# Nine row copies with their own semaphores, and a one-tensor tie step, in stage 1 of an eight-stage transformer kernel

## The reference, cut to what matters

```
att = einsum(q, k) / sqrt(8), causal
S = relu(att[head 0]); S[..., 0] = 0; S = S * (1 - eye)
FF = cumsum(S shifted down one row, axis=rows)       # T x T
att = att - FF                                        # every head
keep = rank of FF in its row (ties by index) < eff_k, or the diagonal
att = where(keep, att, -inf); y = softmax(att) @ v; out = y @ w_proj.T + b
```

## Time and profile before

| | us |
|---|---|
| median of 3 runs | 2910.46 |
| lowest, highest run | 2904.49, 2914.45 |
| the profiled execution's own time | 2907.81 |
| its span in the profile | 2906.0 |

### The profile page before, as it was taken

How to read it: one execution, slowest core, us unless ns; L and a number is a source line. 1 busy time by engine, 2 the same in 40 slices (tenths; PEclk the granted TensorE clock), 3 DMA queues, 4 the chain that set the end, 5 groups by cost and what they waited for, 6 DMA issues and landing times. The chain is left out here.

```text
span 2906.0 us, 73996 instructions
## 1 busy us (share of the span) xinstructions
PE 2553.9 (88%) x30564; PEld 1586.3 (55%) x30564; DVE 1802.5 (62%) x5184; ACT 1796.3 (62%) x3222; POOL 347.1 (12%) x718
## 2 busy tenths in 40 slices
PE   7989788888888999999997999999999999886586
PEld 3668466665665532122113657667667676564355
DVE  6899788777875651000005577787787778653852
ACT  3799565555665269999993266666667667421331
POOL 3100332222220100000000100000000000034025
PEclk8989799999999999999998999999999999897698
DMA  3410001111002011100000000000000000312103
GB/s 118 71 26 2 7 12 17 17 17 17 17 10 55 1 59 54 56 1 1 1 1 17 28 14 8 8 2 7 7 2 8 8 2 2 98 23 40 29 19 55
DMA packets 85111, 68.12 MB, mean 23 GB/s; under 512 B 40776, under 2 KB 73688, under 8 KB 84392
## 3 DMA queue, kind: packets, MB, share of 16 engines
q1 hardware_dynamic: 76328, 57.09, 8.2%
q0 software_dynamic: 8448, 6.30, 1.7%
HBM read 47.21 MB, written 19.96 MB: 23 GB/s over the span
## 5 line engine op out<-in xcount | busy, mean ns | idle before, releaser
L1890 ACT ACTIVATE arena<-ps 128x1024 f32<-128x1024 f32 x512 | 474.1, 1281 | 25.9 <-PE ps L1840 24.0
L1341 DVE CUSTOM_DVE_ANT_0 arena<-ps,arena 128x1024 f32<-128x1024 f32 (+7 forms) x384 | 349.9, 931 | 107.0 <-PE ps L1217 91.1
L2268 DVE CUSTOM_DVE_ANT_0 arena<-ps,arena 128x512 f32<-128x512 f32 (+3 forms) x640 | 371.1, 643 | 26.6 <-PE ps L2132 25.8
L1293 ACT ACTIVATE arena<-ps 128x1024 f32<-128x1024 f32 (+3 forms) x320 | 275.2, 896 | 130.6 <-PE ps L1250 127.0
L2225 ACT ACTIVATE arena<-arena 128x1152 f32<-128x1152 f32 (+15 forms) x256 | 306.4, 1199 | 63.1 <-DVE arena L2268 63.1
L2132 PE MATMUL ps<-arena 64*128 64x512 f32 (+3 forms) x1280 | 270.3, 547 | 3.5 <-ACT arena L2201 1.1
L1851 PE MATMUL ps<-arena 128*32 128x512 f32 x2048 | 273.0, 604 | 0.0
L2163 PE MATMUL ps<-arena 128*64 128x128 f32 x4352 | 262.3, 275 | 0.0
L2163 PEld LDWEIGHTS ps<-arena 128*64 128x64 f32 x4352 | 235.3, 137 | 33.4 <-issue 28.7
L2187 ACT COPY arena<-ps 128x512 f32<-128x512 f32 (+3 forms) x410 | 189.7, 517 | 76.0 <-PE ps L2149 73.7
L1245 PE MATMUL ps<-arena 64*128 64x64 f32 x4352 | 217.0, 232 | 20.4 <-ACT arena L1293 12.2
(11 more groups left out here) (312 smaller groups left out, 4003.9 us busy)
## 6 DMA issues: line engine op xcount, KB each, us to landing
arena<-scr_q SPq DMA_DIRECT2D x256, 32.0 KB
scr_s<-scr_f SPq DMA_DIRECT2D x1, 4096.0 KB, 16.8
arena<-scr_k SPq DMA_DIRECT2D x32, 128.0 KB
arena<-by_head_k SPq DMA_DIRECT2D x16, 192.0 KB
arena<-scr_s SPq DMA_DIRECT2D x16, 192.0 KB, 2.7
arena<-by_head_q SPq DMA_DIRECT2D x28, 96.0 KB
by_head_k<-arena SPq DMA_DIRECT2D x5, 512.0 KB, 4.5
scr_x<-arena SPq DMA_DIRECT2D x2, 1024.0 KB, 5.4
```

The costliest lines, as they stand in the source:

```text
L1293: e.activation(turned_block(u, kc), src, ACT.Exp, scale=-1.0).then_inc(exped, 1)
L1341: e.tensor_tensor_reduce(scored_block(u, g)[:, lo:hi], PS[:, 1024 * (k % 2):1024 * (k % 2) + hi - lo], NF[t][:, lo:hi], -1.0, mxs[:, col - ...
L1890: e.activation(PTR[k % RS], PS[:, at(n):at(n) + 1024], ACT.Sigmoid, scale=float(1 / np.sqrt(8.0))).then_inc(weighed, 1)
L2268: e.tensor_tensor_reduce(slot(u, t, g)[:, lo:hi], PS[:, base(step) + 512 * g:base(step) + 512 * g + hi - lo], bias, -1.0, mxs[:, col - 1:c ...
```

## The change

Two edits. The first makes only the nine copies that a score chunk reads: queries of column block c in bands 1 to c, keys of block c in band c alone, for c of 1 to 3. Their landings are counted on the semaphores `d_q[0..2]`, which later count the query loads of the attention (these waits get an offset), one for each column block; TensorE waits before row tiles 4, 8 and 12 for that block's copies (2, 3 and 4 of them). The second rewrites penalty steps 4 to 6: step 4 has one tensor operand, (count > need) * -TINY, in place of two, and writes `E`; step 5 is (FF - threshold) > that mark, written to `CS`; step 6 reads `CS` for `E`. The planner's costs are as before.

```diff
+TINY = float(2.0 ** -126)
...
-                for c in range(4):
-                    for by, ready, of, to in ((filled, 7 + c, q_rows, q_rows), (qkv_biased, 3 * c + 3, k_t, k_rows)):
-                        w.wait_ge(by, ready)
-                        for g in range(1, 4):
-                            e.dma_start(cols(to, c)[32 * g:32 * g + 8, :], cols(of, c)[0:8, :]).then_inc(d_rows, 16)
+                for c in range(1, 4):
+                    w.wait_ge(filled, 7 + c)
+                    for g in range(1, c + 1):
+                        e.dma_start(cols(q_rows, c)[32 * g:32 * g + 8, :], cols(q_rows, c)[0:8, :]).then_inc(d_q[c - 1], 16)
+                    w.wait_ge(qkv_biased, 3 * c + 3)
+                    e.dma_start(cols(k_rows, c)[32 * c:32 * c + 8, :], cols(k_t, c)[0:8, :]).then_inc(d_q[c - 1], 16)
                 rpe_sync(e, w)
...
                         if g:
-                            w.wait_ge(d_rows, 384)
+                            w.wait_ge(d_q[t // 4 - 1], 16 * (t // 4 + 1))
...
                 if j == 4:
-                    e.scalar_tensor_tensor(CS[:, 0:W], CS[:, 0:W], nd, E[:, 0:W], ALU.is_gt, ALU.mult).then_inc(penalty, 1)
+                    e.tensor_scalar(E[:, 0:W], CS[:, 0:W], nd, -TINY, ALU.is_gt, ALU.mult).then_inc(penalty, 1)
                 if j == 5:
-                    e.scalar_tensor_tensor(E[:, 0:W], nf, th, CS[:, 0:W], ALU.is_gt, ALU.max).then_inc(penalty, 1)
+                    e.scalar_tensor_tensor(CS[:, 0:W], nf, th, E[:, 0:W], ALU.subtract, ALU.is_gt).then_inc(penalty, 1)
                 if j == 6:
-                    e.scalar_tensor_tensor(nf, E[:, 0:W], NEG, nf, ALU.mult, ALU.subtract).then_inc(penalty, 1)
+                    e.scalar_tensor_tensor(nf, CS[:, 0:W], NEG, nf, ALU.mult, ALU.subtract).then_inc(penalty, 1)
...
                         w.wait_ge(d_k, 512)
-                        w.wait_ge(d_q[r % 3], 256 * (r // 3 + 1))
+                        w.wait_ge(d_q[r % 3], 16 * (r % 3 + 2) + 256 * (r // 3 + 1))
```

More of the change, by code:

```diff
@@ L742, in stage1 @@
             q_rows, k_rows = reg(D0 + 13312, 2048), reg(D0 + 15360, 2048)
-            d_rows = sem("f_d_rows")
             def head_rows(g):
```

## The result

The changed kernel takes 2896.15 us (median of 6 runs, 2887.33 to 2898.37) beside 2910.22 us (2899.18 to 2915.03, 6 runs) for the kernel before on the same chip: a ratio of 0.995, with a 95% interval of 0.9932 to 0.9967. It is 14.1 us faster by the medians. The forecast was 2901.3 us in a range of 2894 to 2909. The profiled execution took 2898.27 us against the 2907.8 us of before, 9.5 us less.

A forecast was written before the change was run, and what follows sets the result against it. In the running sums half-clocked TensorE, then VectorE, was taken as the bound; in the attention no engine is full. Copies 4.1 us plus tie step 5.1 make 9.2 us off the median 2910.5: 2901.3 us, range 2894 to 2909.

The forecast's parts named there:

- The copies, 4.1 us: Running sums: TensorE's 4.1 us hole before a product goes away, and everything behind moves forward by as much.
- its lower end: Copies' gain in the running sums: only 2 us if the half-clock stretch lasts longer relative to the work.
- Its sign of being wrong: Running sums: forecast wrong if half clock ends as late as 55 us with VectorE idle as before or more.
- What is late next: Running sums: tile 2's carry is in time, tile 3's starts near 33.3 us, the residual bias load doesn't hold.
- The step's length: Attention's tie step 4: 746 ns at 2048 columns, 546 at 1280; VectorE relieved of 13.0 us; steps 5 and 6 unchanged.
- Where the relief arrives: Attention: 5.1 us of 13.0 reaches the end; tiles 7, 15, 14 in full, 8 gives 0.34, 4 and 5 nothing.
- The term that was mis-sized: tile 15: Attention, tile 15: a shorter step 4 moves GpSimd's split, awaited 3.76 us by TensorE, up in full, 1.60 us.
- The total: Whole kernel: 4.1 us from copies and 5.1 from the tie step, 9.2 us off the median, 2901.3 us.
- Rival A: Running sums: the clock comes back earlier and VectorE's 4.4 us of idle time shrinks; 2897 us, chance 0.15.
- Rival B: Attention: the tie step's relief is hidden by the next wait for ScalarE, only copies count; 2905.4 us, chance 0.27.
- Rival C: Search: starting 4 us earlier, part runs at 1.2 GHz, losing 0.37 us per microsecond; 2919 us and more, chance 0.04.
- Rival D: Running sums: another release ends with the copies, so only the tie step's 5.1 us stay; 2905.4 us, chance 0.05.

The follow-up runs named there:

- the move: Step 5 of tile 15's penalty emitted one unit later; in the changed kernel, with the short step, 2903.02 us, ratio 0.9981 to the kernel before.
- the second one of the same kernel: The changed kernel run once more, nothing altered, on the chip of the two halves: 2896.85 us, ratio 0.9955 to the kernel before.
- The kernel before with the move: The kernel before, old tie step and old copies, with only step 5 of tile 15's penalty emitted one unit later: 2912.98 us, ratio 1.0016.

## Why the prediction was right, step by step

- **The copies, 4.1 us.** Right in size: 4.1 us from carry to mask between two executions of equal half-clock length, 3.6 us by the medians. Not quite by the path forecast: from the first carry to that of tile 3 the kernel gained 5.4 us (10.3 became 4.9), and from there to the mask it lost 1.4 (59.7 became 61.2). In that part the half clock ended later relative to the work, which fits the loss and is what the prediction named as the reason for its lower end. Its sign of being wrong, half clock to 55 us with VectorE idle as before or more, did appear (56.9 us, 6.1 us idle for 4.4), and yet the 4.1 us came: it was a poor sign, since it doesn't add up the whole stretch. The copies were ready early, no new wait took the hole's place, and the last copy was issued at 27.3 us.
- **What is late next.** Right: the carry of tile 3 came at 32.79 for 33.3, its last wait being ScalarE's copy, and the bias load of SyncE's queue held nobody.
- **The step's length.** Right: 750, 547 and 350 ns for 746, 546 and the narrow end; VectorE's busy time fell by 12.3 us (1802.5 to 1790.2) for 13.0 worked out, the 13 instructions themselves by 12.98 (20.14 to 7.17), and steps 5 and 6 were unchanged.
- **Where the relief arrives.** Tile 7 gave 0.80 us for 0.82, and tiles 13, 11, 9, 4 and 5 gave next to nothing, as said. Tile 14 gave 0.74 us for 1.51, tile 8 gave 0.00 for 0.34, and tiles 3, 12, 10 and 6 changed the lead by a few tenths that partly came back. The spacings of the earlier trace rows compared different kinds of unit and were no good guide.
- **The term that was mis-sized: tile 15.** It stood in the sum with 1.60 us and brought 5.45. The wait of 3.76 us in the earlier trace rows was taken as a wait that shortens by what the step shortens. It was two holds in a row, of 2.25 and 2.34 us, and a shorter step 4 takes the split out of reach of step 5, so that nearly the whole wait goes: 3.76 - 0.36 = 3.4 us. The rest, 5.45 - 3.4 = 2.0 us, I put down to the half clock of 6.8 us that followed the wait in the kernel before; this part is argued and not shown. No profiled kernel with the new step at tile 15 and the order of before has half clock there. The kernel with only the copies' change supports the size: its half clock there lasted 10.2 us and its tile 15 took 14.0 us instead of 13.1, so 3.4 us more of half clock cost 0.97 us, and 6.8 us would cost about 1.9 (an estimate from this one pair). That what decides is which splits the steps hold, and not the step's length, is shown by the move, which brought a wait of 4.50 us with the short step in place.
- **The total.** The attention gained 6.8 us in the profiled execution, 9.6 in the second one of the same kernel, for 5.1 forecast. The forecast's gain of 9.2 us lies just outside the first comparison's interval (9.6 to 19.8 us of 2910.22) and just inside the second's (9.0 to 16.9). The tile's surplus of 3.85 us less the 1.1 us that tiles 14 and 8 fell short makes 9.2 + 2.7 = 11.9, and what still lacks to 14 can't be told from scatter. That the 5.1 us came near the 6.8 of the profile is in part luck: tile 15 was put too low, tiles 14 and 8 too high.
- **Rival A** (the clock comes back earlier) is not seen in the profiled execution, where the stretch was 27.3 us again. Other executions had 20.5 and 17.1 us, with and without the hole for the former. It is left open.
- **Rival B** (the relief is hidden) is right for ten of the thirteen steps and wrong for the whole, since three of them carry it. **Rival C** (slower by half clock in the search) didn't occur: the search was 2.2 us shorter. Its price was misread: the row of 43 products in the earlier trace rows ends at 214.3 us and the half clock already at 212.5. The window from 206.8 to 212.5 has 28 products in 5.70 us, 0.203 us each, so a microsecond at half clock loses 0.46 us, not 0.37, and some 39 us of it would have been enough, not 48. Half clock also fell at 96.4 us, where TensorE had stood 3.79 us, and not only behind the 14.48. **Rival D** (no hole filled) fell with the first timeline.

## What to carry to other kernels

Where a GpSimd instruction of 0.2 us lasts 2 us in the timeline, look at what VectorE runs beside it, add up the holds that fall within one chain of GpSimd steps, and set the sum against the work that TensorE still has. Here one hold of 2.25 us cost TensorE 0.36 us, one of 4.26 cost 3.38, and two within one split cost 1.74 to 4.50. Each wait of over 3 us around tile 15 was followed by half clock, and so very likely costs more than its length. Price a shortened or moved step by which neighbour it lets through or holds next, on both sides, and not by its own duration. Where an order is planned from costs, give each kind of step its measured length before shortening any of them.

## What the runs showed of the hardware

- With TensorE busy for all 19.00 us of a window the granted clock stayed at 0.52; the half-clock stretch of the same work lasted 17.1, 20.5, 27.3 or 30.7 us in different executions. The Trainium skill (TensorE: Matmul & The Clock Gate, "What's actually happening") says that activity releases the throttle. In this window, a mix of products with 8 and with 128 rows (L766, L777), TensorE had no idle time and the clock rose only at 56.9 us, so the trace doesn't agree.
- TensorE idle for 2.4 of 3.3 us, or for all of 3.4, was each time followed by half clock, for 6.8 and 10.2 us. The 4.50 us wait of the kernel before with the move was followed by 3.4 us of it, so the length isn't set by the wait alone.
- The new step, with one tensor input in SBUF, still holds a GpSimd cast, for 0.66 us of its 0.75. Casts that start during a step 0 of the penalty, also with one tensor input, take 0.19 or 0.20 us.
- The same program on two chips differed by 24 us (0.8%), more than the whole change brought.
